# A recommendation tower on one core: who marks the first two table units, and where two pair blocks stand

## The reference

```python
e = stack([tbl_f[ids[:, f]] for f in range(26)], axis=1)          # 512 x 26 x 128
sd = einsum('bfd,bd->bf', e, dense); ss = einsum('bfd,bgd->bfg', e, e)
z = concatenate([dense, sd, ss[:, iu, ju]], axis=1)               # pairs i < j
h = concatenate([z, dense], axis=1)
h = maximum(h @ W_top1 + b_top1, 0); h = maximum(h @ W_top2 + b_top2, 0)
y = h @ W_top3                                                    # W: 607x512, 512x256, 256x1
```

## Time and profile before

| | us |
|---|---|
| three runs | 117.4, 117.57, 118.24 (median 117.57) |
| profiled execution | 117.33 |
| its span | 115.3 |
| busy PE / DVE / ACT / POOL | 107.0 / 62.2 / 62.1 / 58.3 |
| granted TensorE clock, mean | 1.00 |

### The profile page before, as it was taken

The page is one execution under the profiler, slowest core; times in us unless marked ns, Lnnn a source line. Parts: engine busy times, 40 slices in busy tenths (PEclk is TensorE's granted clock), DMA queues, the critical chain, the costliest instruction groups (busy, mean ns, idle before and its releaser), DMA issues.

```text
span 115.3 us, 3393 instructions
## 1 busy us (share of the span) xinstructions
PE 107.0 (93%) x1514; PEld 86.8 (75%) x1514; DVE 62.2 (54%) x90; ACT 62.1 (54%) x82; POOL 58.3 (51%) x56
## 2 busy tenths in 40 slices
PE   5979899999999999999999998889999987999991
PEld 4637677868888888888887666768787875989891
DVE  0378998689897799798950007107131026008321
ACT  2379999993999999998930405003121016102220
POOL 0177788777777777788777506006677000000000
PEclk9999999999999999999999999999999999999999
DMA  1897976755766975999312201100212100000000
GB/s 41 248 299 276 287 281 227 244 137 200 275 179 218 347 205 144 374 276 336 84 46 51 67 1 28 28 6 23 50 47 68 28 6 0 6 0 6 6 0 1
DMA packets 6416, 14.84 MB, mean 129 GB/s; under 512 B 2125, under 2 KB 2637, under 8 KB 6402
## 3 DMA queue, kind: packets, MB, share of 16 engines
q1 hardware_dynamic: 4306, 10.94, 28.7%
q0 software_dynamic: 1664, 3.41, 10.7%
q10 hardware_dynamic: 432, 0.27, 0.8%
HBM read 14.62 MB, written 0.00 MB: 127 GB/s over the span
## 4 chain that ended last, share of the span: by engine, by line
PE 66%; ACT 13%; issue 9%; DVE 6%; DMA 4%; ACTq 1%
PE gram_ps L533 11%; PE h_ps L505 9%; PE h_ps L501 8%; PE gram_ps L501 7%; PE gram_ps L505 7%; ACT dist L294 5%; PE h_ps L557 5%; DMA raw<-oh 4%; PE h_ps L550 3%; PE h_ps L580 3%; ACT hi L282 3%; PE h_ps L567 3%; PE turn_ps L521 2%; ACT onehot L297 2%; DVE zfull L431 2%
## 5 line engine op out<-in xcount | busy, mean ns | idle before, releaser
L260 POOL DMA_INDIRECT got<-tbl,ids_sb x52 | 58.1, 1117 | 31.0 <-issue 14.9
L416 DVE TENSOR_SCALAR onehot<-ids_bc,rows_sb 128x1024 fp32r<-128x1024 int16 (+1 forms) x47 | 31.0, 718 | 5.4 <-DMA rows_sb<-rows 3.7
L418 DVE TENSOR_TENSOR lo<-raw,hi 128x1024 fp32r<-128x1024 f32 (+2 forms) x14 | 17.1, 1224 | 4.2 <-ACT hi L282 3.6
L501 PE MATMUL h_ps<-onehot,hi 128*128 128x512 f32 x60 | 16.7, 412 | 1.0 <-ACT onehot L297 0.8
L533 PE MATMUL gram_ps<-vecs 128*27 128x27 f32 x1024 | 13.3, 192 | 2.2 <-issue 1.5
L533 PEld LDWEIGHTS gram_ps<-vecs 128*27 128x27 f32 x1024 | 10.6, 104 | 6.3 <-issue 4.1
L308 ACT ACTIVATE vecs<-turn_ps 128x512 f32<-128x512 f32 (+2 forms) x16 | 8.2, 521 | 12.6 <-PE turn_ps L521 12.6
L505 PE MATMUL h_ps<-onehot,lo 128*128 128x512 f32 x60 | 15.0, 390 | 0.0
L501 PEld LDWEIGHTS h_ps<-onehot,hi 128*128 128x128 f32 x60 | 11.0, 192 | 5.1 <-ACT onehot L297 1.9
L431 DVE STREAM_TRANSPOSE zfull<-gram_ps 128x864 f32<-128x864 f32 x3 | 3.2, 1083 | 21.4 <-PE gram_ps L533 21.4
L297 ACT ACTIVATE onehot<-dist,rows_sb 128x1024 fp32r<-128x1024 f32 (+1 forms) x13 | 14.1, 1087 | 0.4
(11 more groups left out here) (55 smaller groups left out, 87.4 us busy)
## 6 DMA issues: line engine op xcount, KB each, us to landing
raw<-oh SPq DMA_DIRECT2D x8, 512.0 KB, 3.7
raw<-oh SPq DMA_DIRECT2D x4, 640.0 KB, 4.1
ids_bc<-ids_oh SPq DMA_DIRECT2D x6, 256.0 KB, 4.3
got<-tbl,ids_sb POOLq DMA_INDIRECT x52, 3.5
w1p_sb<-w_pairs SPq DMA_DIRECT2D x1, 702.0 KB
w1d_sb<-w_dense SPq DMA_DIRECT2D x1, 512.0 KB
w_sb<-w SPq DMA_DIRECT2D x1, 512.0 KB
raw<-oh ACTq DMA_DIRECT2D x2, 128.0 KB, 4.4
```

The lines of the kernel that those rows point to most:

```text
L260: nc.gpsimd.indirect_dma_start(out=got[:, t, k, :], out_offset=None, in_=tables[k], in_offset=bass.IndirectOffsetOnAxis(ap=ids_sb[:, at:at ...
L416: nc.vector.tensor_scalar(there, row_numbers, rows_sb[:, c:c + 1], None, ALU.is_equal).then_inc(oh_dve, 1)
L418: nc.vector.tensor_tensor(lo[:, u % 2, 0:width(u)], raw[:, u % RAWS, 0:width(u)], hi[:, u % 2, 0:width(u)], ALU.subtract).then_inc(lo_read ...
L501: nc.tensor.matmul(banks[:, s, :], hi[:, u % 2, q * DIM:(q + 1) * DIM], onehot[:, u % 2, q * BATCH:(q + 1) * BATCH], start=(c == 0), stop= ...
```

## The change

In units 0 and 1 ScalarE makes no marks, so VectorE makes all four of each. In TensorE's order, parts 6 and 7 of the gram of tile 1 follow part 5 at once, the pair blocks 1 and 2 of tile 0 come after them, the three unread matmuls around `turn_pairs(1)` go, and pair block 3 of tile 0 stands behind `turn_pairs(1)`. The unread matmul before the gram of tile 1 (L640) stays.

```diff
-ACT_MARKS = [1, 1, 1, 1, 1, 1, 0, 1, 1, 1, 1, 1, 1, 1]
+ACT_MARKS = [0, 0, 1, 1, 1, 1, 0, 1, 1, 1, 1, 1, 1, 1]
...
             gram(1, 5, PARTS)
+            gram(1, 6, PARTS)
+            gram(1, 7, PARTS)
             layer1_pairs_of_tile(0, [1])
-            gram(1, 6, PARTS)
             layer1_pairs_of_tile(0, [2])
-            gram(1, 7, PARTS)
+            turn_group(2, 3)
+            turn_pairs(1)
             layer1_pairs_of_tile(0, [3])
-            turn_group(2, 3)
-            keep_busy(0, 2 * GROUPS + 2)
-            keep_busy(0, 2 * GROUPS + 2)
-            turn_pairs(1)
-            keep_busy(0, 2 * GROUPS + 2)
             layer1_pairs_of_tile(1)
             layer2(0)
             gram(2, 0, PARTS)
```

## The result

The changed kernel took 113.68 us (median; 113.22 to 113.86 in four runs) against 117.91 for the kernel before on the same chip, a ratio of 0.964 (0.958 to 0.969). Two later measurements on other chips gave 0.968 (0.963 to 0.973) and 0.972 (0.967 to 0.976). So it is 3.3 us (by the last ratio) to 4.2 us (by the first medians) faster; I had forecast 2.9 and a range that ended at 113.9. Whether the change makes these dips rarer or the counts fell so by chance, the runs don't show.

A forecast was written before the change was run, and what follows sets the result against it. ScalarE was taken to bound the kernel before 25.60 us, TensorE to 63.30, then TensorE and relays. Terms -1.1 - 1.7 - 0.1 = -2.9 us, from the median 117.57: forecast 114.7, range 113.9 to 116.0.

The forecast's parts named there:

- What bounds: Whole kernel: ScalarE's splits and marks until 25.60 us, TensorE to 63.30, then TensorE alternating with a relay behind each gram.
- Part 1: Look-ups: without ScalarE's marks in units 0 and 1, its later marks come 1.1 us earlier; bounds -0.6 and -1.4.
- The 8.76 for the end of unit 0: Unit 0: TensorE's look-ups finish at 8.76 us, not 9.70, no longer waiting for the mark.
- Its cover by the gathers: POOL's gathers have a reserve, 4.5 us idle before gather 41, so nothing was taken off the marks' gain.
- Part 2: Tile 1: with gram parts 6 and 7 first, its gram completes 1.7 us earlier; bounds -1.8 and -1.4.
- The cover of 3.25 us: Tile 1's relay, from VectorE's transpose to its pair blocks: the moved pair blocks fit within it to 0.05 us.
- The stops, -0.1 us: Gram stages: twelve fewer instructions shift TensorE's later waits for instruction blocks; -0.1 us, bounds -0.4 and +0.6.
- -0.4 at 93 us: Stop at 93.30: three of a dense block's four instructions come in front and cover some 0.35 us; bound -0.4.
- up to +0.6 at 102.7: Stop at 102.69: the block would begin behind a dense block and half a pair block, growing by up to 0.6 us.
- (a): Look-ups: the marks' gain is absorbed by a late table or VectorE's later subtraction; 115.8 us, chance 0.14.
- (b): Tile 1: some 0.8 of the reordering's 1.7 us is left, through stops or late transposes; 115.6 to 116.2, chance 0.08.
- (c): Behind tile 1's gram: unread matmuls hold TensorE's clock, so without them it halves; 121 us, chance 0.03.

The follow-up runs named there:

- p1_marks: Kernel before with only the marks of units 0 and 1 moved to VectorE, TensorE's order kept: 116.69 against 117.61 us (0.994).
- marks5: Changed kernel with ScalarE's one mark in unit 5 also given to VectorE: 114.48 us.
- drop_three: Kernel before without its three unread matmuls around tile 1's pair transposes, nothing else: 117.33 against 117.15 us (1.000).
- after_third: Changed kernel itself, measured again beside three others on the same chip: 113.63 us.
- pad128_start: Changed kernel with 32 tiny unread matmuls (128 instructions) behind those at the start: 119.75 us, 1.019 of the kernel before.
- pad88_start: Changed kernel with 22 tiny unread matmuls (88 instructions) behind those at the start: 117.99 us, 1.002 of the kernel before.
- f1: Changed kernel with pair block 1 moved ahead of gram part 5 of tile 1: 114.11 us (0.971).
- f3: f2 with gram parts 2 and 3 of tile 2 behind layer 2, dense blocks 0 and 1 behind them: 112.61 us (0.964).
- f2: f1 with group (2,3)'s turns also ahead of gram part 5, and tile 2's gram parts 0 and 1 before tile 1's pair blocks: 113.92 us.

## Why the prediction was right and wrong

- **What bounds.** Right: ScalarE before 25.6 us, TensorE to 63, then the relays.
- **Part 1, -1.1 us.** Right in mechanism: -1.0 in the profile, 0.7 to 0.9 in the times of p1_marks, and all intermediate starts within 0.12 us. The 8.76 for the end of unit 0 is not the sum of the terms beside it (7.53 + 4 x 0.23 + 0.10 = 8.55); the row of before, 8.51 to 9.70, gives 8.72, and the trace has 7.55 + 1.20 = 8.75. Its cover by the gathers was thinner than I said (marks5).
- **Part 2, -1.7 us.** The mechanism is right, the size a little low. From the end of the stop to the transpose the kernel before needs 75.52 to 78.36, 2.84 us, the changed one 74.61 to 75.53, 0.92: 1.9 us less. 1.7 are the blocks; 0.2 is the gram itself, which runs faster in one piece (79 matmuls in 0.89 us, before in three pieces of together 1.09). The cover of 3.25 us held to 0.01 us.
- **The stops, -0.1 us. This step failed.** I took -0.4 at 93 us and set against it up to +0.6 at 102.7. The -0.4 came (tile 1's transpose to tile 2's: 16.05 and 15.97 before, 15.66, 15.63 and 15.76 after, 15.65 in drop_three). The growth did not: tile 2's transpose to tile 3's takes 10.40 us with a stop of 0.25 and 10.16 without one in the two profiles of before, 10.43 with one and 10.17 without in the changed kernel (its third, 10.47, has 3.4 us of halved clock). I had the work right: between the boundaries 2497 and 2753 lie 2.73 us of it instead of 3.37. What I had wrong is when the block is ordered. The growth of 0.6 lets it arrive a fixed time after TensorE passes the boundary before, which I had said that no row shows. Its packet starts 1.32 and 0.92 us after that in the two profiles of before, but 0.28 in all three of the changed kernel: about as much earlier as the work is shorter. Over all profiles without pads at the start it is 0.27 to 0.29 us in the 11 without the twelve instructions and 0.91 to 1.32 in the 5 with them. What orders the packet, the traces don't show.
- **Where the rest of the profiled pair comes from.** My terms gave 114.4 for the profiled execution; it took 113.86. Of the 0.55 us, 0.3 are the stop term, 0.2 the gram in one piece, and 0.4 two stops (at 102.69 and in tile 0's gram) that happen to be missing. Against them stand 0.1 of part 1 and 0.25 of stops around 1473 that happen to be longer. The last two entries on stops are luck.
- **The step to the median.** I set the sum against 117.57, because the median lay 0.24 us above the profiled execution. In the changed kernel's four runs the profiled one is the slowest, and the median lies 0.18 below it. That takes another 0.4 us off, and so the median falls 0.2 below my range. A sum with the terms as measured (-1.0, -1.9, -0.4) gives 114.2 to 114.3 from 117.57, inside it.
- **Rivals.** (a) did not decide: hi of unit 2 waited for the look-ups, not for its table. (b) did not, (c) did not: the span's clock is 1.00. The Trainium skill's rule on transposes (TensorE: Matmul & The Clock Gate, Part 4: PE-mode transpose), by which (c) would have been likelier, is not borne out: 16 of the 18 profiles run the transposes behind tile 2's gram at clock 1.00. In the two others (after_third, pad128_start) the clock is at 0.50 there, but falls before the transposes start. The Trainium skill's rule that block crossings are mostly hidden (Runtime: NRT & Kernel Launch, Instruction fetch mechanics) holds in the look-ups, where 256 instructions take some 26 us, and fails in the grams, by 1.8 us in the changed kernel and 5.4 in pad88_start.

## What to carry to other kernels

Where many small matmuls follow each other, count the engine's instructions as well as its work: look for idle time that nothing ends, check whether it recurs at a fixed number and behind a packet of the instruction queue, and put slow matmuls ahead of it, where they are free (f1's chain, f3). When a block of work is moved out from between two others, ask at its old place what it covered (f2's h2) and, where an engine gets ahead, which transfers run at their own pace (marks5). Set a sum against like runs, and take more than one profile of the kernel before if its runs spread more than the terms in dispute.

## What the runs showed of the hardware

TensorE's instructions came in blocks of 256. In 60 of 61 stops it went on 1.23 to 1.60 us after the end of the block's 16 KB packet, whose start lay 0.2 to 1.9 us behind the boundary before. From one boundary to the instruction behind the next it took 2.7 to 4.1 us where a stop stood (4.5 and 4.7 once each); a stretch with less work than that could stop, up to 2.1 us in pad128_start. It need not: at 961 and at 2753 TensorE passed with 2.57 and 2.73 us of work behind it and no stop in some profiles, when the packet came early.

The granted clock (1.00 is the 2.4 GHz level) fell to 0.50 for some us at a time in three of the 18 profiles: in pad128_start some 15 us behind two stops of 2.1 and 1.7 us, while tile 2's gram ended and the transposes behind it ran; in after_third at the same work (90.1 to 93.5), where it cost about 0.4 us; and in drop_three in the first look-ups from about 7.9 us on, about when TensorE's wait for unit 0's last mark began. The rows are those of pad128_start and of drop_three (columns as in the earlier trace rows):

```profile
95.10:98.40 3.30, 3.30 (x45) 3.02 (x46) 2.03 (x3) 1.41 (x3) 0.00 (x0) 0.50 0.00 0
```

```profile
7.90:14.60 6.70, 5.89 (x15) 4.57 (x15) 5.30 (x9) 5.89 (x8) 5.18 (x6) 0.50 0.81 246
```

What sets it off, these runs don't show. The first tables landed up to 0.7 us apart from run to run: ScalarE's hi of unit 0 started between 5.21 and 5.89 us, in kernels that are the same up to there on ScalarE and on the queues.
